# First image of an eight-image network kernel: normalising chunk by chunk, splitting a scale exchange, and moving weight halves to GpSimd

## What is computed

```
x = x + relu(W0 [GN(x), 25 local correlations of GN(x)] + b0)       (layer 0)
x = x + silu(Wout (scan(conv(silu(Win GN(x)))) * gate + res) + bout) (layer 1)
x = x + W2 GN(x) + b2                                               (layer 2)
x = x + W3 GN(x) + b3                                               (layer 3)
```

## Time and profile before

| | |
|---|---|
| three runs | 1723.71, 1725.22, 1725.95 us; median 1725.22 |
| the profiled execution | 1724.77 us |
| its span | 1722.9 us, granted TensorE clock 0.988 of full |
| TensorE busy | 1637.4 us, 95% |
| VectorE busy | 1169.0 us, 68% |
| ScalarE busy | 890.2 us, 52% |
| GpSimd busy | 402.6 us, 23% |

### The profile page before, as it was taken

One profiled execution on the slowest core, in us unless ns is written; L12 is line 12 of the kernel. 1 busy time (PEld: TensorE's weight loads), 2 busy tenths in 40 slices (PEclk: granted clock), 3 DMA queues, 4 the chain that ended last, 5 costly groups with the idle time before them and its releaser, 6 DMA issues.

```text
span 1722.9 us, 24375 instructions
## 1 busy us (share of the span) xinstructions
PE 1637.4 (95%) x8661; PEld 920.4 (53%) x8661; DVE 1169.0 (68%) x2480; ACT 890.2 (52%) x1091; POOL 402.6 (23%) x418
## 2 busy tenths in 40 slices
PE   4588999999999999999999999999999999999987
PEld 3254654556545655456545565455554565545643
DVE  6779776567755676548775578556775577653865
ACT  4647453475355653555544754457525564446532
POOL 1304311043021431223220430204302142113310
PEclk9789999999999999999999999999999999999999
DMA  6303410244102431224212441024310242112301
GB/s 206 99 0 105 147 28 14 74 134 143 41 23 84 126 119 41 75 73 147 76 22 74 129 147 28 17 78 142 128 40 34 85 138 96 39 49 79 113 12 49
DMA packets 140718, 140.17 MB, mean 81 GB/s; under 512 B 68899, under 2 KB 118115, under 8 KB 140590
## 3 DMA queue, kind: packets, MB, share of 16 engines
q1 hardware_dynamic: 126542, 103.18, 19.5%
q0 software_dynamic: 12288, 34.68, 6.2%
q10 hardware_dynamic: 1760, 0.64, 0.2%
HBM read 78.46 MB, written 60.01 MB: 80 GB/s over the span
## 4 chain that ended last, share of the span: by engine, by line
PE 82%; DVE 11%; issue 3%; ACT 3%; DMA 1%; POOL 0%; DVEq 0%; SPq 0%; POOLq 0%; ACTq 0%
PE bank L1632 77%; PE bank L1800 2%; PE bank L1933 2%; DVE bn L921 1%; DVE gate L1144 1%; PE bank L1852 1%; DVE scan_tmp L1504 1%; ACT L719 1%; DMA x_even<-in_x 1%; ACT work L573 1%; DVE wmax L891 0%; DVE work L1584 0%; ACT buf_a L570 0%; PE bank L1702 0%; DVE scan_tmp L1506 0%
## 5 line engine op out<-in xcount | busy, mean ns | idle before, releaser
L1632 PE MATMUL bank<-buf_a,win_hi 128*128 128x512 f16 x1536 | 460.7, 382 | 8.2 <-DVE buf_a L993 8.1
L1632 PE MATMUL bank<-buf_a,win_lo 128*128 128x512 f16 x768 | 292.5, 381 | 0.0
L1632 PE MATMUL bank<-buf_b,w_hi 128*128 128x512 f16 x960 | 286.7, 380 | 2.5 <-DVE buf_b L993 2.5
L1632 PEld LDWEIGHTS bank<-buf_a,win_hi 128*128 128x128 f16 x1536 | 148.5, 99 | 174.7 <-DVE buf_a L993 10.9
L471 POOL DMA_INDIRECT d_scan<-rows,rank x128 | 126.5, 988 | 347.2 <-ACT rows L654 304.6
L1632 PE MATMUL bank<-buf_b,w_lo 128*128 128x512 f16 x480 | 182.4, 380 | 0.0
L487 POOL DMA_INDIRECT rows<-d_y,rank x128 | 129.1, 1008 | 203.7 <-DMA d_y<-buf_b 168.2
L1632 PE MATMUL bank<-buf_a,w_hi 128*128 128x512 f16 x576 | 171.3, 379 | 2.2 <-DVE x_odd L1236 2.1
L1632 PEld LDWEIGHTS bank<-buf_b,w_hi 128*128 128x128 f16 x960 | 93.7, 99 | 111.9 <-DVE buf_b L993 3.2
L1632 PEld LDWEIGHTS bank<-buf_a,win_lo 128*128 128x128 f16 x768 | 75.5, 98 | 91.9 <-issue 2.2
L1632 PE MATMUL bank<-gate,w_out 128*128 128x512 f32 x256 | 120.3, 603 | 1.1 <-DVE gate L1349 1.1
(11 more groups left out here) (256 smaller groups left out, 3058.9 us busy)
## 6 DMA issues: line engine op xcount, KB each, us to landing
rows<-d_scan SPq DMA_DIRECT2D x16, 1024.0 KB, 5.9
d_y<-buf_b SPq DMA_DIRECT2D x64, 256.0 KB, 2.4
work<-in_x SPq DMA_DIRECT2D x24, 512.0 KB, 4.6
d_gram<-rows SPq DMA_DIRECT2D x32, 260.0 KB, 2.4
x_even<-in_x SPq DMA_DIRECT2D x16, 512.0 KB, 6.6
x_odd<-in_x SPq DMA_DIRECT2D x16, 512.0 KB, 5.5
out_x<-x_even SPq DMA_DIRECT2D x16, 512.0 KB, 2.9
out_x<-x_odd SPq DMA_DIRECT2D x16, 512.0 KB, 2.6
```

What stands on the lines that cost most here:

```text
L1632: return eng.matmul(out, lhsT, rhs, start=start, stop=stop, skip_group_check=True, **kw)
```

## The change

Only the first image's order changes; in the others some semaphore targets are renumbered, since the first image now counts more steps in the second normalisation.

1. The second normalisation of image 0 goes by chunk on VectorE, GpSimd, ScalarE and TensorE, with the functions of the last image. VectorE's splits of chunks 0 and 1 stand between its units; ScalarE normalises chunk 0 ahead of its evacuation of unit 7. TensorE takes the first five units of the projection chunk by chunk, and chunk 3's group sum behind the first products of two units.
2. The third exchange is cut into `collect` (the transpose, now behind two units after tokens(1) instead of one) and `spread` (the broadcast), now behind tokens(3). VectorE's part after `spread` stands behind convolution 3.
3. ScalarE first scales L2's and L3's weights in place and then rounds them to high halves, sixteen operations; GpSimd subtracts (eight, `rest_lows`) between the scatters of head 0 and head 1. VectorE's `rest_lows` goes.
4. The zeroed pad and the zeroed stage count on one semaphore.

```
 per-image targets:
+        FIRST_BY_CHUNK = dict(gn_stat1=2 * KC - 2, gn_sum1=KC - 1, gn_var1=3 * KC - 3, gn_rstd1=KC - 1, gn_bias1=KC - 1)
-                eng.wait_ge(s[name], m * per[name] + n)
+                eng.wait_ge(s[name], m * per[name] + n + (0 if is_first(m) else FIRST_BY_CHUNK.get(name, 0)))
 GpSimd, image:
                 for h in range(HEADS):
+                    if first and h:
+                        rest_lows()
                     if first:
                         eng.wait_ge(s["p_rank"], h + 1)
...
+            def rest_lows():
+                for name in ("L2", "L3"):
+                    for n, (k, v) in enumerate(wchunks[name]):
+                        eng.wait_ge(s["w_hi_" + name], KC + n + 1)
+                        eng.tensor_tensor(w_lo[name][:, k, :], v, w_hi[name][:, k, :], ALU.subtract).then_inc(s["w_lo_late"], 1)
...
-            l0_adds(0, 0)
-            rstd(0, 1)
+            for k in range(KC):
+                l0_add(0, 0, 2 * k)
+                if k >= 2:
+                    chunk_rstd(0, 1, k - 2)
+            chunk_rstd(0, 1, KC - 2)
+            chunk_rstd(0, 1, KC - 1)
 ScalarE:
                     for k, v in wchunks[name]:
-                        act(w_hi[name][:, k, :], v, ACT.Copy, scale=scale(name)).then_inc(s["w_hi_" + name], 1)
+                        act(v, v, ACT.Copy, scale=scale(name)).then_inc(s["w_hi_" + name], 1)
+                    for k, v in wchunks[name]:
+                        eng.wait_ge(s["w_hi_" + name], k + 1)
+                        act(w_hi[name][:, k, :], v, ACT.Copy).then_inc(s["w_hi_" + name], 1)
...
             for u in range(3, 8):
                 l0_evac(0, u)
+                if u == 6:
+                    normalize(0, 1, 0, X[0], True)
             in_weights(3)
-            for k in range(KC):
-                normalize(0, 1, k, X[0])
+            for k in range(1, KC):
+                normalize(0, 1, k, X[0], True)
 VectorE (chunk_moments and chunk_bias skip the shift where g < 2):
-                scales(2, 4, 2)
+            def rest_bounds(between):
+                scales(2, 4, 2, between)
...
+                for k in range(KC - 1):
+                    convolve(k)
+                if first:
+                    rest_bounds(lambda: convolve(KC - 1))
+                else:
+                    convolve(KC - 1)
...
                 if first:
-                    rest_lows()
-                    eng.wait_ge(s["w_lo_rest"], 2 * KC + 2)
+                    eng.wait_ge(s["w_lo_late"], 2 * KC)
...
             for u in range(8):
                 l0_unit(0, 0, u)
-                if u % 2 and u > 1:
-                    aggregate(0, 1, u // 2 - 1)
-            aggregate(0, 1, KC - 1)
-            moments(0, 1)
-            variance(0, 1)
-            bias(0, 1)
-            for k in (2, 3):
+                if u % 2:
+                    chunk_moments(0, 1, u // 2, 3 * (u // 2) + 2)
+                    if u > 1:
+                        chunk_bias(0, 1, u // 2 - 1)
+                if u >= 4 and u % 2 == 0:
+                    split(0, 1, u // 2 - 2)
+            def in_low(k):
                 eng.wait_ge(s["w_hi_in"], k + 1)
                 eng.wait_ge(s["w_lo_in"], k)
                 low("in", k, wchunks["in"][k][1]).then_inc(s["w_lo_in"], 1)
-                split(0, 1, k - 2)
+            in_low(2)
+            chunk_bias(0, 1, KC - 1)
             split(0, 1, 2)
+            in_low(3)
             split(0, 1, 3)
 TensorE:
+                    if first and k == 0 and q == 1:
+                        chunk_sum(m, 1, KC - 1)
-                steps = iter([(q, k) for q in range(24) for k in range(KC)])
+                steps = iter([(q, k) for k in range(KC) for q in range(5)] + [(q, k) for q in range(5, 24) for k in range(KC)]
+                             if first else [(q, k) for q in range(24) for k in range(KC)])
...
                 tokens(1)
+                filler(2)
                 if first:
-                    filler(1)
-                    exchange(2, 4, lambda: filler(1))
-                else:
-                    filler(2)
+                    collect(2, 4)
                 tokens(2)
                 piece(KC + 1)
                 tokens(3)
+                if first:
+                    spread(2, 4)
                 piece(5 * KC - 1)
...
-            gn_sum(0, 1)
+            for k in range(KC - 1):
+                chunk_sum(0, 1, k)
             images(eng, image)
```

More of the change, by code:

```diff
@@ L206, in build @@
             p_abcd p_sqrt p_count p_zero p_score p_rank a_in a_exp x_in x_out early_in
[L207 removed]
+            w_lo_late pad_out gram_mm gram_d norm_t norm_max norm_pow norm_row norm_out norm_in norm_m gram_ev gram_pad
             gram_out0 gram_out1 gram_out2 gram_out3 gram_in corr_msk corr_t corr_cp corr_lo
@@ L309, in _ @@
             weights("in")
-            eng.wait_ge(s["pad_zero"], 1)
+            eng.wait_ge(s["w_corrz"], 2)
             eng.dma_start(bass.AP(d_norm.tensor, d_norm.offset, [[N + REACH, 2], [1, REACH]]), zero_pad).then_inc(s["pad_out"], 16)
@@ L403, in _ @@
             eng.memset(corr_stage, 0.0).then_inc(s["w_corrz"], 1)
-            eng.memset(zero_pad, 0.0).then_inc(s["pad_zero"], 1)
+            eng.memset(zero_pad, 0.0).then_inc(s["w_corrz"], 1)
             eng.memset(minus_half, -0.5).then_inc(s["half_in"], 1)
@@ L417, in chunk_rstd @@
             def chunk_rstd(m, g, k):
-                wait(eng, f"gn_var{g}", m, 4 * k + 3)
+                wait(eng, f"gn_var{g}", m, (4 if g >= 2 else 3) * k + 3)
                 eng.tensor_tensor(st[g][:, k:k + 1, 4], st[g][:, k:k + 1, 3], minus_half, ALU.pow).then_inc(s[f"gn_rstd{g}"], 1)
@@ L947, in chunk_moments @@
                 wait(eng, f"gn_raw{g}", m, raw + 1)
-                TT(mean, mean, shift[:, g - 2, k:k + 1], ALU.subtract).then_inc(s[f"gn_stat{g}"], 1)
-                wait(eng, f"gn_stat{g}", m, 3 * k + 1)
+                n = (3 if g >= 2 else 2) * k
+                if g >= 2:
+                    TT(mean, mean, shift[:, g - 2, k:k + 1], ALU.subtract).then_inc(s[f"gn_stat{g}"], 1)
+                    n += 1
+                    wait(eng, f"gn_stat{g}", m, n)
                 TT(sq, mean, mean, ALU.mult).then_inc(s[f"gn_stat{g}"], 1)
-                wait(eng, f"gn_stat{g}", m, 3 * k + 2)
+                wait(eng, f"gn_stat{g}", m, n + 1)
                 TT(second, second, sq, ALU.add).then_inc(s[f"gn_stat{g}"], 1)
@@ L956, in chunk_bias @@
                 mean, second, sq, var, rs, off = (st[g][:, k:k + 1, j] for j in range(6))
+                n = (4 if g >= 2 else 3) * k
                 wait(eng, f"gn_sum{g}", m, k + 1)
                 eng.tensor_copy(st[g][:, k, 0:2], gn_ps[g][:, k, :]).then_inc(s[f"gn_var{g}"], 1)
-                wait(eng, f"gn_var{g}", m, 4 * k + 1)
+                wait(eng, f"gn_var{g}", m, n + 1)
                 TT(sq, mean, mean, ALU.mult).then_inc(s[f"gn_var{g}"], 1)
-                wait(eng, f"gn_var{g}", m, 4 * k + 2)
+                wait(eng, f"gn_var{g}", m, n + 2)
                 STT(var, second, EPS, sq, ALU.add, ALU.subtract).then_inc(s[f"gn_var{g}"], 1)
-                TT(mean, mean, shift[:, g - 2, k:k + 1], ALU.add).then_inc(s[f"gn_var{g}"], 1)
-                wait(eng, f"gn_var{g}", m, 4 * k + 4)
+                if g >= 2:
+                    TT(mean, mean, shift[:, g - 2, k:k + 1], ALU.add).then_inc(s[f"gn_var{g}"], 1)
+                    wait(eng, f"gn_var{g}", m, n + 4)
                 wait(eng, f"gn_rstd{g}", m, k + 1)
@@ L1099, in y_low @@
                     ALU.mult, ALU.subtract).then_inc(s["y_lo"], 1)
-            def rest_lows():
-                for name in ("L2", "L3"):
-                    for n, (k, v) in enumerate(wchunks[name]):
-                        eng.wait_ge(s["w_hi_" + name], n + 1)
-                        low(name, k, v).then_inc(s["w_lo_rest"], 1)
             def small_factors():
@@ L1246, in image, with convolve @@
                 first = is_first(m)
-                for k in range(KC):
+                def convolve(k):
                     if first and k == 0:
@@ L1635, in exchange, with collect, spread @@
             def exchange(rnd, n, between=None):
+                collect(rnd, n)
+                if between:
+                    between()
+                spread(rnd, n)
+            def collect(rnd, n):
                 eng.wait_ge(s["w_maxc"], rnd + 1)
                 eng.transpose(ps[7][0:n, 0:P], par[:, WMAX:WMAX + n], ident).then_inc(s["w_maxt"], 1)
-                if between:
-                    between()
+            def spread(rnd, n):
                 eng.wait_ge(s["w_maxr"], 2 * rnd + 2)
@@ L1649, in chunk_sum @@
             def chunk_sum(m, g, k):
-                wait(eng, f"gn_stat{g}", m, 3 * k + 3)
+                wait(eng, f"gn_stat{g}", m, (3 if g >= 2 else 2) * (k + 1))
                 if k:
-                    wait(eng, f"gn_var{g}", m, 4 * k - 3)
```

(1 more changed line is left out.)

1 line of the change is left out of this document (removed).

## The result

The changed kernel takes 1736.09 us (median of five runs, 1732.60 to 1737.75) beside 1724.76 for the kernel before (five runs on the same chip): ratio 1.006, 95% interval 1.0047 to 1.0072. A second set of four runs gave 1736.19, ratio 1.0072 (1.0047 to 1.0096). The forecast was 1729.8, range 1725 to 1734: the direction is right, the size is too small by 6 us, and the time lies outside the range. The profiled execution took 1737.62, span 1735.7.

A forecast was written before the change was run, and what follows sets the result against it. VectorE's queue in the first image was taken to set the time up to `row_ready`, then one chain through GpSimd's scatters and the load. Delayed scan sums 3.8 plus port 1.2 gave +5.0, 1729.8 us, range 1725 to 1734.

The forecast's parts named there:

- Second normalisation on VectorE, +7.3: First image: VectorE's fourth split ends at 90.6 against 83.35, with two waits of about 2.5 for ScalarE.
- first tap holds VectorE 1.0: Second convolution: if half clock lasts to 92, TensorE's second unit ends at 97.7 and VectorE loses 1.0.
- TensorE gains little: Projection units: first product moves from 76.6 to about 75.0, but chunk 3's sum waits for unit 7's statistics, 81.7.
- tokens at full clock: Exchange sum: the tokens' product and transposes ahead of the transposed maxima counted at 2.6 us.
- Exchange, -3.3: Third exchange: waits of 7.7 plus 2.8 for tokens 3 become 6.7 plus 0.5; `row_ready` 4.0 to 5.0 late.
- the fourth rival: Exchange is not off VectorE's path but moved behind tokens 3; already in the sum, no chance given.
- Low halves, sums +3.8 and port 1.2: GpSimd subtractions at 1.1 delay head 1's scatters 8.2, second masks 7.1, TensorE's scan sums 3.8; port contention adds 1.2.
- From there the first image is one chain: Behind TensorE's second group of scan sums, the first image has no slack.
- if later images change length: Sign of being wrong: later images keep their orders, so their length should not change.
- head 1 waits for a contended GpSimd: Rival 1: last four subtractions at 1.66 (+2.2), or half clock until 99; +6.5 to +9, 1731 to 1734, chance 0.18.
- The second's smaller cost: Rival 2: chunk order costs VectorE 3 to 6 instead of 7.8; 0 to +3, 1725 to 1728, chance 0.2.
- The third: Rival 3: chunk order free, exchange and low halves count in full; -3.3 to -8.7, 1716 to 1721.5, chance 0.1.

The follow-up runs named there:

- the first execution: The changed kernel, unaltered, first profiled execution: 1737.62 us; second image starts at 207.08, last stretch 301.4.
- the second execution: The changed kernel profiled once more, unaltered: 1732.79 us; second image starts at 203.51, last stretch 301.4.

## Why the prediction was wrong in size

- **Second normalisation on VectorE, +7.3:** right. 90.44 for 90.6, with both waits. The added "first tap holds VectorE 1.0" didn't come: the second convolution ends 7.05 later.
- **"TensorE gains little" and tokens at full clock:** the step that failed first. I followed the units only to ask whether they would be late. They were early, so TensorE stood 6.1 us, went to half clock and reached the exchange's transpose late. The sum had nothing for this; the normalisation alone shows +2.4 behind the +7.1, with tokens 0 at 3.63 us for the 1.87 that I had put in.
- **Exchange, -3.3:** right by itself, -3.8 by the ratio, with the new wait for the broadcast that the fourth rival names (5.02 for 4.3); in the changed kernel `row_ready` comes 3.4 earlier than with the normalisation alone (138.44, there some 141.85). With the missed 2.4 it comes 6.2 late instead of 4.0 to 5.0.
- **Low halves, sums +3.8 and port 1.2:** the chain is right (low halves, scatters, load, masks), and so are the 1.1 for a subtraction alone and about 1.2 for the port on GpSimd (measured 1.11 and 1.0). The term that is too small is what lies behind: the forecast moved the scatters and the load along unchanged, and in the first execution they took 0.9 and 1.3 us more. With `row_ready` 1.6 later than forecast and the low halves 0.6 quicker than its sum, these make about the 3.1 us by which the sums came later than forecast, 8.1 for 5.0. In the second execution they came 6.1 late. The 3.4 us of port on VectorE, which I had not seen, end in its wait for the rows. The forecast had the low halves at about nothing; measured by themselves they are +1.7.
- **"From there the first image is one chain":** true, but not at one speed. In the first execution half clock behind TensorE's idle 4.0 us cost 1.5 more.
- **I am wrong "if later images change length":** they did in both executions, 2.4 us in the last. No step of mine spoke of it, and whether it belongs to the change is not shown.
- **Rivals.** The first (head 1 waits for a contended GpSimd, 1731 to 1734) was nearest; its place is right, its reasons aren't: contended subtractions took 1.24 and not 1.66, the clock was back by 88 and not at 99, and the time went behind the subtractions. That its range lies next to the result is luck. The second's smaller cost needs another order: with units first it is 3.3. The third falls, its condition being a fourth split by 83.

The 11 us of the median are then: 7.1 normalisation, 2.4 TensorE behind it, -3.4 exchange, 0 to 3.5 low halves, scatters and the clock at the scan, 2.4 last image. These make 8.5 to 12; the two profiled spans are 8.1 and 12.8 longer than that of before, with -0.4 and 0.7 in the six images between. The first three are shown by runs of their own, the fourth only by rows of two executions, the last is seen but not explained.

## What to carry to other kernels

Ask of an engine not only whether it will be late but also whether it will be early: a TensorE that runs ahead stands idle, and its next work, at half clock, may hold what the other engines wait for. Filling that gap with useless products did not pay here. Cutting an exchange in two pays by where its two ends stand in TensorE's queue: ahead of the units it was worth 12 us by the ratio, behind them 4. Work moved to GpSimd fits only into its real gap, here four of eight low halves; what reaches beyond is paid in the scatters and in the load behind them. And a difference of 2 to 4 us in 1725 can't be read from one profiled execution: the exchange alone started its second image at 195.94 once and at 192.86 the next time.

## What was not expected of the hardware

- A scatter issue of GpSimd took 1.92 or 1.49 us instead of 0.96 beside VectorE's products of two SBUF operands, one or two in eight: 1.91 or 1.92 beside the product of 128x1024 in five executions of three kernels, but only 1.02 beside VectorE's low halves in the kernel before.
- The same kernel's first image was 3.6 us longer in one execution than in another, through one stretched scatter, the load behind it and half clock after a gap of 4.0 us that was 1.47 in the other.
- After the same idle time of 1.76 us in the last image the granted clock fell to half in both executions of the changed kernel and in none of the three of the kernel before; with the low halves alone it fell in one execution and not in the other.
- Keeping TensorE busy over 6 us moved the half-clock stretch from between 100 and 110 us to between 111 and 114.
